# Cross-attention with a mixture of experts on one core: short clears on GpSimd behind each row transfer, and a wait ahead of every second result transfer

## The chip, the cores and the metric

The kernel runs on one core of a Trainium2 chip. Its engines work side by side and wait for each other through semaphores: TensorE (PE, with its weight loads as PEld), VectorE (DVE), ScalarE (ACT), GpSimd (POOL) and SyncE (SP). The metric is the device time of one execution in microseconds, the lower the better. A comparison is given as a ratio with an interval.

## What is computed

All numbers are float32. There are 64 sequences of 64 tokens with 256 features, so 4096 tokens. A layer norm is followed by cross-attention of each sequence over its context and itself, and by a mixture of 32 experts of which each token uses 4, beside a shared feed-forward network. Both parts are added to the residual.

```
x = x + attention(layernorm(x), keys/values = [ctx, layernorm(x)], wq, wk, wv, wo)
h = layernorm(x)
probs = softmax(h @ router.T);  topv, topi = top_k(probs, 4);  topv /= sum(topv)
out = sum over the 4 chosen experts e:  topv_e * ((silu(h @ w_gate[e]) * (h @ w_up[e])) @ w_down[e])
shared = (silu(h @ sw_gate) * (h @ sw_up)) @ sw_down
x = x + out + sigmoid(h @ sgate_w) * shared
```

An expert is 256 by 96 (gate and up) and 96 by 256 (down). The shared network is 512 wide.

## The kernel before

The tokens are cut into 16 blocks of 256 (two tiles of 128 rows) and, for the shared network, into 8 groups of 512. Each engine has its own program, written out by hand. The order on an engine is that of its code, and nothing but semaphores orders the engines among each other.

**Attention.** A loop over n runs from block to block as a pipeline: in step n, TensorE computes the projections of block n (line 806, three products for each, of a high and a low part), the attention of block n-1, the transposes and the router's logits of block n-3 (line 1012), and the places of the tokens in the experts' lists for block n-4 (lines 1021 and 1023). ScalarE copies the logits out of PSUM (line 616), and VectorE makes of them the four experts, their weights (line 1289, semaphore `weights_ready`) and the row in DRAM to which each token's copy goes (`slot_ready`). The last four steps of the loop, n = 16 to 19, carry the shared products of group 0 in place of projections. The shared products of groups 1 to 3 stand behind the loop (lines 806 and 850), and behind them the experts begin.

**The row transfers.** For each block GpSimd issues eight indirect DMAs, one for each of two tiles and four choices, which scatter 128 rows of 268 words from the buffer `rows` to `sent` in DRAM (line 481). It waits for `weights_ready`, `slot_ready` and two more of that block. `rows` is a ring of six blocks, so block b+6 is normalized into it only when the transfers of block b have landed. There are 128 such transfers. Behind some of them GpSimd runs `breathe`: it clears one of four small tiles `pause` (128 by 24, line 490), each clear waiting for the clear four before it. In the loop on GpSimd this is one clear, and only where n > 16. The transfers left behind the loop have three clears each. By the code 92 transfers have none, 24 have one and 12 have three.

**The experts.** The sorted rows make 136 tiles of 128, worked through as 68 pairs. SyncE may load from `sent` only when all row transfers have landed and the tables are made (lines 417 and 419). TensorE's loop for a pair is: transposes of pair + 2 (line 1049), transposes of the activations of pair - 1 (line 1111), gate and up products of pair + 1 (line 1100, and 1096 for pairs whose first tile mixes four experts), and the down product of pair - 3 (line 1128, and 1125 for the mixed ones), whose last matmul raises `worked_psum`. ScalarE applies silu (line 737), VectorE multiplies (line 1580), copies the transposed activations (line 1586) and scales the down product into `down_e` (line 1597, `down_ready`), a ring of four pairs that it refills once both transfers of the pair four before have landed. The call `worked(pair)` is the count at which the down product of that pair is done.

**The result transfers.** For each pair GpSimd waits for `back_ready` and `down_ready`, and then issues two indirect DMAs from `down_e` to `returned` in DRAM (line 512), one right behind the other. When all have landed, SyncE loads them back in 16 pieces, VectorE folds them into the residual (lines 1698, 1701 and 1705), and TensorE runs the shared products of groups 4 to 7 beside that (lines 806, 850 and 840).

## Time and profile before

| what | us |
|---|---|
| median of 3 runs | 516.37 (515.13 to 516.96) |
| profiled execution, its span | 667.5 |
| of that, PE busy | 574.4 |
| DVE busy | 363.5 |
| ACT busy | 288.7 |
| POOL busy | 269.4 |

The profiled execution is one execution, taken with the hardware profiler. Its span is the only time of it that is at hand, and it is 151 us longer than the median of the runs. So a time that is read in the trace can't be taken over to the runs one to one. Times in the trace count from the start of the span. "Idle before" in a row is the time that the engine waited ahead of the instruction, and the name behind the arrow is the instruction that released it. "remote" and "issue" mean that the trace shows no such instruction at that time.

### The profile page before, as it was taken

The page shows a single profiled execution, that of the slowest core. Times are in us where ns is not written, and L with a number is a line of the kernel's source. Part 1 is how long each engine was busy: PE and PEld are TensorE (multiplying, and loading weights), DVE is VectorE, ACT ScalarE, POOL GpSimd, SP SyncE. Part 2 cuts the span into 40 slices and gives each one's busy share as a digit, 9 for nine tenths or more (in the row PEclk, how much of TensorE's full clock was granted, in tenths as well). Part 3 has the DMA queues.
Part 4 walks back from the last instruction along what each step waited for, and adds up shares of the span by engine and source line. Part 5 has one row for each costly group of instructions (what it writes and reads, how often), then busy time and mean ns, then how long its engine had stood idle before and what let it go on. Part 6 is the DMA issues. An engine that isn't in the chain of part 4 may idle for free. (4 is left out here: it accounts for less than half of the span.)

```text
span 667.5 us, 13365 instructions
## 1 busy us (share of the span) xinstructions
PE 574.4 (86%) x3945; PEld 478.3 (72%) x3945; DVE 363.5 (54%) x1199; ACT 288.7 (43%) x719; POOL 269.4 (40%) x344
## 2 busy tenths in 40 slices
PE   8998787788887777899998988778877898979998
PEld 7997777677777565677886666656666676658886
DVE  5575455555555351565553635445454444536998
ACT  5775444555444440613463545444454544401111
POOL 1004444445555458380034544445454454560000
PEclk9999788987778788699997977988989978989999
DMA  5573544444433322293145444544444544228996
GB/s 160 181 227 128 170 156 129 144 134 145 138 123 113 110 76 107 70 244 98 31 130 148 131 140 124 140 136 139 130 140 140 150 131 132 87 86 330 368 340 230
DMA packets 65956, 100.77 MB, mean 151 GB/s; under 512 B 9856, under 2 KB 52864, under 8 KB 65792
## 3 DMA queue, kind: packets, MB, share of 16 engines
q1 hardware_dynamic: 48704, 60.30, 30.6%
q0 software_dynamic: 12672, 35.41, 14.7%
q10 hardware_dynamic: 4512, 4.23, 1.9%
q8 instruction: 34, 0.56, 0.4%
q14 instruction: 34, 0.28, 0.1%
HBM read 55.92 MB, written 43.97 MB: 150 GB/s over the span
## 5 line engine op out<-in xcount | busy, mean ns | idle before, releaser
L512 POOL DMA_INDIRECT returned<-arena,back x136 | 130.6, 960 | 171.7 <-DVE back L1629 81.5
L481 POOL DMA_INDIRECT sent<-rows,slot x128 | 129.9, 1015 | 159.2 <-issue 82.7
L1100 PE MATMUL bank<-w_gu,arena 128*128 x416 | 94.7, 363 | 26.6 <-issue 16.6
L1100 PEld LDWEIGHTS bank<-w_gu,arena 128*128 128x128 f32 x416 | 73.0, 205 | 32.8 <-issue 32.8
L1580 DVE TENSOR_TENSOR arena<-bank,arena 128x192 f32<-128x192 f32 x68 | 24.2, 356 | 113.5 <-ACT arena L737 94.5
L737 ACT ACTIVATE arena<-bank 128x192 f32<-128x192 f32 x68 | 22.3, 329 | 127.0 <-remote 70.5
L806 PE MATMUL bank<-w_hi_all,att_split 128*128 128x256 f32 x256 | 56.8, 314 | 18.6 <-issue 18.6
L1597 DVE TENSOR_SCALAR arena<-bank,back_to 128x256 f32<-128x256 f32 x136 | 59.0, 476 | 6.3 <-remote 5.3
L806 PE MATMUL bank<-att_split,w_hi_all 128*128 128x256 f32 x256 | 55.5, 336 | 1.4 <-issue 1.3
L710 ACT COPY hnt<-w_gu 128x384 f32 x128 | 55.7, 509 | 0.0
L806 PEld LDWEIGHTS bank<-w_hi_all,att_split 128*128 128x128 f32 x256 | 42.4, 208 | 18.2 <-issue 18.2
L806 PE MATMUL bank<-hnt_rounded,ws_hi 128*128 128x512 f32 x160 | 51.0, 412 | 2.6 <-issue 2.6
L806 PEld LDWEIGHTS bank<-att_split,w_hi_all 128*128 128x128 f32 x256 | 47.7, 248 | 4.7 <-issue 4.6
L539 ACT ACTIVATE act_t<-bank 128x512 f32<-128x512 f32 x24 | 14.2, 598 | 82.9 <-PE bank L806 66.6
L1049 PE MATMUL bank<-ident_r,loaded 128*128 128x128 f32 x272 | 46.0, 295 | 0.4 <-issue 0.4
L850 PE MATMUL bank<-ws_d,act_t 128*128 128x256 f32 x192 | 43.3, 381 | 1.0 <-DVE act_t L1241 1.0
L731 ACT COPY arena<-bank 128x512 f32<-128x512 f32 x68 | 39.5, 582 | 8.9 <-PE bank L1049 2.5
L850 PEld LDWEIGHTS bank<-ws_d,act_t 128*128 128x128 f32 x192 | 36.1, 190 | 6.4 <-DVE act_t L1241 1.4
L806 PEld LDWEIGHTS bank<-hnt_rounded,ws_hi 128*128 128x128 f32 x160 | 31.6, 197 | 10.9 <-issue 4.0
L1049 PEld LDWEIGHTS bank<-ident_r,loaded 128*128 128x128 f32 x272 | 32.6, 148 | 9.0 <-issue 2.8
L806 PE MATMUL bank<-w_lo_all,att_split 128*128 128x256 f32 x128 | 30.3, 310 | 6.8 <-issue 6.5
L1311 DVE TENSOR_REDUCE negmax<-bank 128x2 f32<-128x256 f32 x16 | 6.7, 422 | 51.8 <-remote 51.8
(216 smaller groups left out, 1128.6 us busy)
## 6 DMA issues: line engine op xcount, KB each, us to landing
arena<-returned SPq DMA_DIRECT2D x16, 1024.0 KB, 7.2
loaded<-sent SPq DMA_DIRECT2D x104, 134.0 KB
w_gu<-w_gate_up SPq DMA_DIRECT2D x32, 192.0 KB
sent<-rows SPq DMA_DIRECT2D x4, 1072.0 KB, 6.2
loaded<-sent SPq DMA_DIRECT2D x128, 33.5 KB
resid<-x SPq DMA_DIRECT2D x16, 256.0 KB, 2.9
att_plain<-ctx_t SPq DMA_DIRECT2D x16, 256.0 KB, 3.1
out<-resid ACTq DMA_DIRECT2D x7, 512.0 KB, 4.9
```

The lines of the kernel that those rows point to most:

```text
L481: pool.indirect_dma_start(out=sent, out_offset=bass.IndirectOffsetOnAxis(ap=slot[:, 2 * b + j, k:k + 1], axis=0), in_=rows[:, u, j, :], in ...
L512: pool.indirect_dma_start(out=returned, out_offset=bass.IndirectOffsetOnAxis(ap=back[:, t:t + 1], axis=0), in_=down_e[u][:, s, :], in_offs ...
L539: act.activation(act_t[:, f, :], gate_banks[f % 2][:, :], ACT.Silu) \
L710: last = act.copy(gu_copy[:, q, :, :], w_gu[:, :, bass.ds(copied_e[pair][q], 1), :] .rearrange("p c e f -> p c (e f)"))
L731: act.copy(gt[pair % 2].rearrange("p s c q -> p (s c q)"), gt_banks[pair % 2][:, :]) \
L737: act.activation(act_e[pair % 2], gu_views[pair % 2][:, :, 0:F], ACT.Silu) \
L806: last = pe.matmul(out_view, stationary(s_part, c), moving(m_part, c), start=(n == 0 and c == 0), stop=(n == 2 and c == DC - 1))
L850: last = pe.matmul(sum_banks[t // 2][:, 256 * (t % 2):256 * (t % 2) + 256], act_t[:, f, P * t:P * t + P], ws_d[:, f, :], start=(f == 0 and ...
L1049: last = pe.transpose(gt_banks[pair % 2][:, at:at + P].bitcast(F32R), loaded[:, u, s, P * c:P * c + P], ident_r[:, :])
L1100: last = pe.matmul(view[:, s, :], rows_t[:, s, c, :], w_gu[:, c, bass.ds(e[s - 2 + len(e)], 1), :] .rearrange("p e f -> p (e f)"), start=( ...
L1580: dve.tensor_tensor(act_e[pair % 2], gu_views[pair % 2][:, :, F:2 * F], act_e[pair % 2], ALU.mult).then_inc(S["act_e_ready"], 1)
L1597: last = dve.tensor_scalar(down_e[u][:, s, :], down_banks[pair % 2][:, D * s:D * s + D], back_to[:, pair // 2 % 4, 2 * (pair % 2) + s, 0:1 ...
```

## The change

On GpSimd alone, two things. In the attention loop each row transfer is followed by three clears of `pause`, in every step and not one clear in the last steps. In the experts the second result transfer of a pair waits until the down product of the next pair is done. The last pair has no such wait.

```diff
@@ -497,8 +497,7 @@
                 for turn in range(SENT_A_STEP):
                     if may_send(n - 6 if turn < 4 else n - 5):
                         send()
-                        if n > blocks:
-                            breathe(1)
+                        breathe(3)
             while sent_now[0] < len(sends):
                 send()
                 breathe(3)
@@ -509,6 +508,8 @@
                 wait(pool, "down_ready", pair + 1)
                 for s in range(2):
                     t = 2 * pair + s
+                    if s == 1 and pair + 1 < pairs:
+                        wait(pool, "worked_psum", worked(pair + 1))
                     pool.indirect_dma_start(
                         out=returned,
                         out_offset=bass.IndirectOffsetOnAxis(ap=back[:, t:t + 1], axis=0),
```

What stands on GpSimd where the row transfers begin, before (`sent` is the DRAM buffer of the rows, `slot` the places, names in brackets are the semaphores waited for):

```order
L461 IOTA lanes_after 128x1
L463 MEMSET ones_e 32x128
L481 DMA sent<-rows,slot 131200x268 [waits named_ready,weights_ready,numbered,slot_ready,no_rows,consts]
L481 DMA sent<-rows,slot 131200x268 [waits weights_ready,named_ready,slot_ready,numbered,no_rows] x7
L481 DMA sent<-rows,slot 131200x268 [waits weights_ready,slot_ready,named_ready,numbered] x85
L490 MEMSET pause 128x24
```

The same place on GpSimd after the change:

```order
L463 MEMSET ones_e 32x128
L481 DMA sent<-rows,slot 131200x268 [waits named_ready,weights_ready,numbered,slot_ready,no_rows,consts]
L490 MEMSET pause 128x24 x3
L481 DMA sent<-rows,slot 131200x268 [waits weights_ready,named_ready,slot_ready,numbered,no_rows]
L490 MEMSET pause 128x24
L490 MEMSET pause 128x24 [waits breath] x2
L481 DMA sent<-rows,slot 131200x268 [waits weights_ready,named_ready,slot_ready,numbered,no_rows]
L490 MEMSET pause 128x24 [waits breath] x3
```

Ahead of the first clear there were 93 row transfers in a row, and now there is one. No transfer has moved past another.

On GpSimd where the last row transfers end and the result transfers of the experts begin, before:

```order
L481 DMA sent<-rows,slot 131200x268 [waits weights_ready,slot_ready,named_ready,numbered]
L490 MEMSET pause 128x24 [waits breath] x3
L512 DMA returned<-arena,back 36864x256 [waits down_ready,back_ready]
L512 DMA returned<-arena,back 36864x256
L512 DMA returned<-arena,back 36864x256 [waits down_ready,back_ready]
L512 DMA returned<-arena,back 36864x256
```

The same place after the change:

```order
L481 DMA sent<-rows,slot 131200x268 [waits weights_ready,slot_ready,named_ready,numbered]
L490 MEMSET pause 128x24 [waits breath] x3
L513 DMA returned<-arena,back 36864x256 [waits down_ready,back_ready]
L513 DMA returned<-arena,back 36864x256 [waits worked_psum]
L513 DMA returned<-arena,back 36864x256 [waits down_ready,back_ready]
L513 DMA returned<-arena,back 36864x256 [waits worked_psum]
```

The order is the same, and every second transfer now has a wait of its own for a product of TensorE.

## Rows read from the trace of the kernel before

**Rows 1.** Windows: us; busy time and instructions of each engine; granted clock; DMA.
```profile
0.00:56.00 56.00, 53.15 (x453) 49.31 (x454) 34.65 (x118) 38.66 (x97) 2.89 (x20) 1.00 0.59 188
56.00:230.00 174.00, 139.05 (x1002) 123.86 (x1002) 90.86 (x368) 80.79 (x224) 89.77 (x88) 0.82 0.42 135
230.00:300.00 70.00, 58.99 (x262) 46.09 (x261) 33.98 (x127) 24.41 (x45) 46.16 (x100) 0.88 0.41 121
300.00:337.00 37.00, 35.65 (x201) 30.68 (x200) 19.20 (x51) 15.25 (x28) 0.00 (x0) 1.00 0.28 74
337.00:602.00 265.00, 224.72 (x1754) 175.55 (x1753) 128.23 (x460) 120.73 (x313) 130.59 (x136) 0.90 0.44 130
602.00:667.50 65.50, 62.83 (x282) 52.84 (x280) 56.62 (x79) 8.84 (x14) 0.00 (x0) 1.00 0.87 321
```

**Rows 2.** Timeline of PE: start us, us, what. The logits, once a block.
```profile
51.30 1.08 PE L1012 MATMUL bank<-wr,hnt 128*128 128x33 f32 x8
60.91 1.08 PE L1012 MATMUL bank<-wr,hnt 128*128 128x33 f32 x8
76.83 1.08 PE L1012 MATMUL bank<-wr,hnt 128*128 128x33 f32 x8 [0.64 <-ACT hnt L653]
92.33 1.08 PE L1012 MATMUL bank<-wr,hnt 128*128 128x33 f32 x8 [0.79 <-ACT hnt L653]
...
217.92 1.08 PE L1012 MATMUL bank<-wr,hnt 128*128 128x33 f32 x8
```

**Rows 3.** Timeline of ACT: its copy of the logits of 60.91.
```profile
68.14 0.21 ACT L616 COPY logits<-bank 128x66 f32<-128x66 f32 x1 [5.24 <-remote]
```

**Rows 4.** Timeline of POOL: row transfers without clears.
```profile
56.22 1.24 POOL L481 DMA_INDIRECT sent<-rows,slot  x1 [52.48 <-issue]
...
64.20 0.96 POOL L481 DMA_INDIRECT sent<-rows,slot  x1 [0.30 <-issue]
65.47 0.96 POOL L481 DMA_INDIRECT sent<-rows,slot  x1 [0.30 <-issue]
71.70 0.96 POOL L481 DMA_INDIRECT sent<-rows,slot  x1 [5.28 <-DVE rows L1289]
```

**Rows 5.** Timeline of POOL: with one clear, and with three.
```profile
263.58 0.97 POOL L481 DMA_INDIRECT sent<-rows,slot  x1 [0.17 <-issue]
264.54 0.14 POOL L490 MEMSET pause<- 128x24 f32 x1
264.85 0.97 POOL L481 DMA_INDIRECT sent<-rows,slot  x1 [0.17 <-issue]
...
282.83 2.19 POOL L481 DMA_INDIRECT sent<-rows,slot  x1 [0.16 <-issue]
...
288.15 0.97 POOL L481 DMA_INDIRECT sent<-rows,slot  x1 [0.16 <-issue]
289.11 0.25 POOL L490 MEMSET pause<- 128x24 f32 x3
289.52 0.97 POOL L481 DMA_INDIRECT sent<-rows,slot  x1 [0.16 <-issue]
...
297.70 0.97 POOL L481 DMA_INDIRECT sent<-rows,slot  x1 [0.16 <-issue]
```

**Rows 6.** Timeline of ACT behind the run of 16 transfers with one clear.
```profile
268.59 0.59 ACT L653 COPY hnt<-bank 128x512 f32<-128x512 f32 x1 [16.79 <-remote]
```

**Rows 7.** Timeline of PE: down products of the experts.
```profile
336.08 1.03 PE L1128 MATMUL bank<-arena 96*128 x4
338.99 1.13 PE L1128 MATMUL bank<-arena,slot_prod 96*128 x4
341.77 1.03 PE L1128 MATMUL bank<-arena,hnt 96*128 x4
...
585.78 0.70 PE L1128 MATMUL bank<-arena,hnt 96*128 x2
593.30 1.12 PE L1128 MATMUL bank<-arena,slot_prod 96*128 x4 [3.19 <-DVE arena L1597]
```

**Rows 8.** Timeline of DVE: the copy that the product of 585.78 releases.
```profile
592.28 1.66 DVE L1597 TENSOR_SCALAR arena<-bank,back_to 128x256 f32<-128x256 f32 x4 [5.33 <-remote]
```

**Rows 9.** Timeline of POOL: result transfers near the end.
```profile
588.34 0.96 POOL L512 DMA_INDIRECT returned<-arena,back  x1 [0.30 <-issue]
589.60 0.96 POOL L512 DMA_INDIRECT returned<-arena,back  x1 [0.30 <-issue]
593.92 0.95 POOL L512 DMA_INDIRECT returned<-arena,back  x1 [3.36 <-DVE arena L1597]
...
600.24 0.96 POOL L512 DMA_INDIRECT returned<-arena,back  x1 [0.30 <-issue]
```

**Rows 10.** Timelines of SP and PE: the first load, transposes and expert product.
```profile
303.79 0.38 SPq L417 DMA_DIRECT2D loaded<-sent  x1
...
324.27 0.98 PE L1049 MATMUL bank<-ident_r,loaded 128*128 128x128 f32 x8
...
326.89 1.46 PE L1100 MATMUL bank<-w_gu,arena 128*128 x8
```

**Rows 11.** Chain of work that ended last: start us, us, what.
```profile
611.13 10.90 PE bank L806 x48
```

**Rows 12.** Timeline of DVE: product among clears, first fold, last product.
```profile
295.68 0.69 DVE L1241 TENSOR_TENSOR act_t<-bank,act_t 128x512 f32<-128x512 f32 x1 [1.85 <-remote]
...
607.73 1.23 DVE L1698 TENSOR_TENSOR arena<-arena 128x1024 f32<-128x1024 f32 x1 [2.71 <-DMA arena<-returned]
...
659.43 0.68 DVE L1241 TENSOR_TENSOR act_t<-bank,act_t 128x512 f32<-128x512 f32 x1
```

## The prediction, made before the changed kernel was run

> **What bounds the kernel now.** I read the windows first, with edges where GpSimd begins and ends its transfers [rows 1]. In the three stretches without transfers (0 to 56, 300 to 337, 602 to 667.5; 158.5 us together) the granted clock is 1.00, the 2.4 GHz level, and TensorE is busy 151.6 of 158.5 us. In the three with transfers (509 us) the clock is granted at 0.82 to 0.90, so TensorE spends part of its time at the 1.2 GHz level, and it is idle 35, 11 and 40 us. So I asked the timeline what changes when transfers begin. One matmul group stands once in every block, the logits. It comes at 51.30 and 60.91, 9.6 us apart, and then at 76.83 and 92.33, 15.5 apart, up to 217.92 [rows 2]. From 60.91 to 217.92 are ten steps, 15.7 us each. The transfers began at 56.22 [rows 4].
>
> What delays the step is in the rows around it. The logits end on TensorE at 61.99 (60.91 + 1.08), but ScalarE starts to copy them at 68.14, after an idle of 5.24 us that the trace can only call remote [rows 3]. GpSimd's run of eight transfers went from 56.22 to 66.43 [rows 4]. The same at 268.59: ScalarE waited 16.79 us, and it moved 2.8 us behind the last transfer of a run of 16, which began at 264.85 [rows 5, 6]. And at the end of the experts: the down product of 585.78 is over by 586.5, yet VectorE's copy of it starts at 592.28, again released by "remote", while GpSimd issued transfers until 590.56 [rows 7 to 9]. My reading: in this trace TensorE's signals to the other engines do not arrive while GpSimd issues transfers back to back; they come 1 to 3 us after the run ends. A step of attention then is the run (8 x 1.27 = 10.1 us) plus some 5.5 us of the chain that leads to the next run.
>
> The decisive question is how much of this the timed runs have, since they take 151 us less than the span. I sum what the delays cost in the trace. Attention: 10 x (15.7 - 9.6) = 61 us. Experts: the down products run 2.9 and 2.8 us apart before the transfers hinder (336.08, 338.99, 341.77), and 257.2 us for 67 pairs, 3.84 each, over the whole stage [rows 7]: 67 x (3.84 - 2.85) = 66 us. The stretch 230 to 300: 11 us idle, and at a granted 0.88 a quarter of the 70 us at the lower level, which costs half of 17 us: 19 us together [rows 1]. The sum is 146, and 667.5 - 146 = 521.5 us, 5 us above the median of 516.4. So the timed runs behave like the trace without the delays, bound by TensorE nearly throughout. What may be left of delays in them is small: the dense stretches could be somewhat faster unprofiled (48 matmuls of 512 columns take 10.90 us, 227 ns each [rows 11], where 512 columns at 2.4 GHz are 213, so 6% of 158 us, 9 us at most). That puts the timed run without any delay between 512 and 521, and leaves 0 to about 5 us for delays.
>
> The Trainium skill, page "Runtime: NRT & Kernel Launch", section on the preamble/postamble breakdown, says that a profile's total time and the execution time differ by some 6 us whatever the kernel. This case's numbers disagree: 667.5 against 516.4. By that rule the timed run would carry all of the delays, and the change could be worth tens of us; the measurement decides against it.
>
> **The change part by part.** *The clears.* Without a clear a transfer follows the one before after 1.27 us (64.20 to 65.47) [rows 4]. With one clear it is also 1.27 (263.58 to 264.85): the clear lies in the 0.30 us gap. With three it is 1.37 (288.15 to 289.52) [rows 5]. So the 92 + 24 transfers that had none or one each cost 0.10 us more on GpSimd, 11.6 us in all, 0.8 per block. None of that is on the path by itself: VectorE needs a block's buffer only six blocks later. Per block GpSimd needs 8 x 1.37 = 11.0 us where TensorE's undelayed step takes 9.6, so GpSimd falls behind by 1.4 us per block (before: 0.5), some 14 us at the ninth block, the last for whose buffer anyone waits, against about 3 steps (29 us) of room. It is cover until the loads of the experts. There I count: first transfer at 56.2, the 128th 127 x 1.37 = 174 us later at 230, if it never waits; before, 127 x 1.27 gives 217.5. In the trace the first load stands 6.1 us behind the last transfer (297.70 to 303.79) [rows 5, 10]; some 2 us for it to land makes 238. That is an estimate. It must be there for the first transposes, which stand 2.6 us ahead of the first expert product [rows 10]. In the timed run that product comes at 516.4 - (667.5 - 326.9 - 66) = 242, so the transposes at 239. The cover holds by about a us, where it was 14. Cost taken: 0, bounds 0 and +5.
>
> A clear might also hold up VectorE beside it. Its product of 128 by 512 takes 0.69 us at 295.68, among the triple clears, and 0.68 us at 659.43, where GpSimd is idle [rows 12], so 0 for that.
>
> Whether the clears let signals through: with one clear in the gap they did not (16.79 us of waiting [rows 6]). Where three stood (282 to 299) the step shape is different and no row proves it. In the timed run I take 0, bound -2.
>
> *The wait in the experts.* It holds 67 transfers until the next pair's down product, about 2.85 us after this pair's own. GpSimd then has, per pair, the held transfer right at that signal and the first transfer of the next pair behind it: 2 x 1.27 = 2.5 us of 2.85, in step with TensorE. Queued behind the waiting transfer on GpSimd is only the next pair's first one, whose data is ready about 1 us after the same signal (VectorE's copy), so it loses at most 0.3 us. The other one who waits is VectorE's copy into the ring of four: it needs this transfer landed 4 x 2.85 = 11.4 us after this pair's copy; the transfer now starts 2 us behind that copy rather than 1.27 and lands some 2 us later. Seven us of room: cost 0. The end of the stage: the last transfers start at 593.92, six of them in a row until 600.24 [rows 9]. Now the held one of the pair before stands at their head, seven in all, but it can start at the product's signal and not at the copy's end, 0.9 us earlier. 1.27 - 0.9 = 0.4 us later at the first fold, which VectorE already waits for by 2.71 us [rows 12]. VectorE's last product comes at 659.43 behind folds, and a shift of 0.4 has about 2 us of room on TensorE. So 0, bound +0.5.
>
> What the wait can give: in the trace it stops runs longer than two transfers, so a signal is held for 2.5 + 1 us rather than up to 10. I expect the trace's pair to fall from 3.84 to about 3.4 us, 30 us of the span. In the timed run only the 0 to 5 us that are left can be won.
>
> Sum for the timed run: 0 (clears) + 0 (wait) + 0 to 0.4 (end), on 516.4: forecast 516.2, no change.
>
> **The rivals.** *A: the timed run has a rest of the delay, and the change removes it.* TensorE's signals would be late by up to one transfer (0.96 us) here and there. For it: the trace shows the effect at full size. Against: the sum above reaches the median without it. After the change a pair's two transfers lie right behind TensorE's signal and GpSimd is idle when the next one comes. Price: of the 5 us left, plus up to 5 where the dense stretches are faster than I think, most goes: 511, at best 506.
>
> *B, slower: the backlog reaches the experts.* The clears move the last row transfer from 217.5 to 230, and my cover was 1 us. If a step of attention is shorter than 9.6 us in the timed run, or the load of the 3 MB down weights holds transfers up (one took 2.19 us in the trace [rows 5]), every us beyond goes into the start of the experts one to one. It decides from a last transfer at about 232. Price: 2 to 6 us, so 520.
>
> *C, slower: the delay is there in attention's timed steps and scales with the run.* Then each run of eight is 0.8 us longer and some 11 steps are bound by it: +9 us, 525. Against it: the same sum as above.
>
> *D: the clears do not separate the transfers at all,* and the wait is always already met. This gives 516.4, the same as my forecast.
>
> **How the numbers follow.** Forecast (with D) 0.42, A 0.31, B 0.18, C 0.09. A measurement of this kernel can tell about 0.3% from no change, 1.5 us. Same is the forecast: 0.42. Faster is A: 0.31. Slower is B and C: 0.27. The range reaches to A's 508 and to B's 522; beyond it lie A's far end and C.
>
> **What would show it.** In the profile of the changed kernel: row transfers 1.37 us apart all through attention; the logits 16 us or more apart while transfers run (if the clears let signals through, 12 or less); down products about 3.4 us apart; no more than two or three result transfers in a row; ScalarE's and VectorE's remote waits in the experts shorter. A span that falls by 20 us with a median that stays is what I expect. The forecast is wrong if the median follows the span, or if the last row transfer comes too late for the first load.

## The result, and the profile after

The changed kernel took 521.91 us (519.89 to 522.69, 4 runs), the kernel before beside it 515.75 us (512.42 to 516.96, 4 runs): 1.0136 times as long, 95% interval 1.0084 to 1.0189. It is slower, by about 6 us. The ratios of this document leave out the disturbed executions of a set, and the medians are over all of them.

The page of the changed kernel. The profiled execution took 522.01 us, its span is 519.8, 2.2 us less.

```profile
span 519.8 us, 13689 instructions
PE 506.7 (97%) x3945; PEld 431.2 (83%) x3945; DVE 363.5 (70%) x1199; ACT 287.4 (55%) x719; POOL 290.3 (56%) x668
PEclk9999999999999999998999999999999999999999
```

The same windows as in [rows 1], but cut off at this span's end (us; busy time of PE, PEld, DVE, ACT, POOL; granted clock; DMA share; GB/s):

```profile
0.00:56.00 56.00, 53.42 (x452) 49.58 (x453) 34.64 (x118) 38.71 (x97) 2.89 (x20) 1.00 0.59 188
56.00:230.00 174.00, 173.62 (x1336) 154.73 (x1335) 134.93 (x521) 109.99 (x278) 153.94 (x503) 1.00 0.59 183
230.00:300.00 70.00, 67.31 (x554) 55.42 (x553) 40.00 (x136) 39.66 (x97) 31.26 (x41) 0.98 0.54 153
300.00:337.00 37.00, 36.16 (x335) 28.76 (x333) 23.26 (x85) 24.07 (x64) 24.17 (x27) 1.00 0.62 181
337.00:519.00 182.00, 176.16 (x1276) 142.72 (x1274) 130.71 (x342) 74.97 (x186) 78.06 (x81) 1.00 0.67 225
```

Where [rows 1] has 139 busy us of 174 at a clock of 0.82, this has 173.6 at 1.00, while GpSimd is busy for 154 of the 174. The logits, to be laid beside [rows 2], come every 9.6 us (timeline of PE):

```profile
60.98 1.08 PE L1013 MATMUL bank<-wr,hnt 128*128 128x33 f32 x8
70.59 1.08 PE L1013 MATMUL bank<-wr,hnt 128*128 128x33 f32 x8
80.20 1.08 PE L1013 MATMUL bank<-wr,hnt 128*128 128x33 f32 x8
```

ScalarE copies them 0.2 us after they end, not 6 as in [rows 3], with no wait put down to "remote" (timeline of ACT):

```profile
62.21 0.22 ACT L617 COPY logits<-bank 128x66 f32<-128x66 f32 x1 [0.56 <-PE bank L1024]
```

So nothing is left of the 146 us of held signals in this trace. It looks as if the change had removed them. It had not: a profile of the unchanged kernel, taken later (before_b, below), has none either. TensorE is now 97% busy. Of the 13.1 us that it is idle, 2.6 lie in the first 56 us, and nearly all of the rest at the start of the experts and behind it. The last row transfers (timeline of POOL), the first load (SP), and TensorE beside them (PE):

```profile
230.31 0.97 POOL L481 DMA_INDIRECT sent<-rows,slot  x1 [0.16 <-issue]
231.27 0.24 POOL L490 MEMSET pause<- 128x24 f32 x3
231.68 0.97 POOL L481 DMA_INDIRECT sent<-rows,slot  x1 [0.16 <-issue]
```

```profile
235.24 0.38 SPq L417 DMA_DIRECT2D loaded<-sent  x1
```

```profile
238.18 0.50 PE L1050 MATMUL bank<-ident_r,loaded 128*128 128x128 f32 x4 [1.06 <-DMA loaded<-sent]
239.56 0.53 PE L1050 MATMUL bank<-ident_r,loaded 128*128 128x128 f32 x4 [0.88 <-DMA loaded<-sent]
239.93 3.65 PE L851 MATMUL bank<-ws_d,act_t 128*128 128x256 f32 x8
243.38 1.50 PE L1101 MATMUL bank<-w_gu,arena 128*128 x8
```

TensorE waits twice for the loads, 1.94 us. Behind that the clock falls to its 1.2 GHz level for 3.4 us (a window of the same trace, the clock is the 0.50), so the L851 group takes 3.65 us where it takes 1.96 elsewhere:

```profile
240.00:243.40 3.40, 3.40 (x11) 2.65 (x10) 0.00 (x0) 0.59 (x1) 0.00 (x0) 0.50 0.31 78
```

### The profile page after: what moved, and what is told of

Same layout as the page of the kernel before. It is cut to its first block and busy times, and to the rows that moved or that the text cites. A ratio compares the mean times of both kernels' runs of the same rounds, so it can differ in the third digit from the quotient of the medians.

```text
span 519.8 us, 13689 instructions
## 1 busy us (share of the span) xinstructions
PE 506.7 (97%) x3945; PEld 431.2 (83%) x3945; DVE 363.5 (70%) x1199; ACT 287.4 (55%) x719; POOL 290.3 (56%) x668
## 5 line engine op out<-in xcount | busy, mean ns | idle before, releaser
L481 POOL DMA_INDIRECT sent<-rows,slot x128 | 125.8, 983 | 72.6 <-issue 70.1
L1101 PE MATMUL bank<-w_gu,arena 128*128 x416 | 83.6, 338 | 0.8 <-ACT arena L732 0.4
L1101 PEld LDWEIGHTS bank<-w_gu,arena 128*128 128x128 f32 x416 | 66.0, 190 | 1.5 <-issue 1.3
L807 PE MATMUL bank<-w_hi_all,att_split 128*128 128x256 f32 x256 | 48.6, 292 | 0.0
L1050 PE MATMUL bank<-ident_r,loaded 128*128 128x128 f32 x272 | 41.7, 276 | 5.2 <-DMA loaded<-sent 5.2
L851 PE MATMUL bank<-ws_d,act_t 128*128 128x256 f32 x192 | 44.7, 391 | 0.0
L807 PE MATMUL bank<-att_split,w_hi_all 128*128 128x256 f32 x256 | 44.4, 286 | 0.0
L732 ACT COPY arena<-bank 128x512 f32<-128x512 f32 x68 | 39.6, 582 | 5.9 <-PE bank L1050 4.6
L851 PEld LDWEIGHTS bank<-ws_d,act_t 128*128 128x128 f32 x192 | 37.2, 195 | 5.4
L807 PEld LDWEIGHTS bank<-w_hi_all,att_split 128*128 128x128 f32 x256 | 37.1, 191 | 0.9 <-issue 0.9
L807 PEld LDWEIGHTS bank<-att_split,w_hi_all 128*128 128x128 f32 x256 | 37.0, 194 | 0.2
L490 POOL MEMSET pause<- 128x24 f32 x384 | 31.2, 142 | 0.0
L1097 PE MATMUL bank<-hnt,arena 128*32 128x192 f32 x512 | 27.4, 332 | 0.0
```

Of the source, the lines that this page charges most:

```text
L481: pool.indirect_dma_start(out=sent, out_offset=bass.IndirectOffsetOnAxis(ap=slot[:, 2 * b + j, k:k + 1], axis=0), in_=rows[:, u, j, :], in ...
L490: pool.memset(pause[breaths[0] % len(pause)][:, :], 0.0).then_inc(S["breath"], 1)
L732: act.copy(gt[pair % 2].rearrange("p s c q -> p (s c q)"), gt_banks[pair % 2][:, :]) \
L807: last = pe.matmul(out_view, stationary(s_part, c), moving(m_part, c), start=(n == 0 and c == 0), stop=(n == 2 and c == DC - 1))
L851: last = pe.matmul(sum_banks[t // 2][:, 256 * (t % 2):256 * (t % 2) + 256], act_t[:, f, P * t:P * t + P], ws_d[:, f, :], start=(f == 0 and ...
L1050: last = pe.transpose(gt_banks[pair % 2][:, at:at + P].bitcast(F32R), loaded[:, u, s, P * c:P * c + P], ident_r[:, :])
```

## The experiments

**Two conditions of the chip.** The kernels ran in five sets, those of a set on one chip beside the kernel before. The kernel before had a median of 515.23 us in the second set and 516.86 in the fourth, but of 653.38, 669.88 and 660.44 in the first, third and fifth. In the three long sets the traces show the held signals of [rows 3, 6]; in the two short ones there are none. I call these sets held and free. The set of the first result, above, was free too. The third (held) and the fourth (free) ran under the same chip number, eight minutes apart. Held times scatter by up to 4%, so a held ratio says less than a free one, and its median stands beside it.

**First set (held): the parts, one by one.** The clears alone:

```
-                        if n > blocks:
-                            breathe(1)
+                        breathe(3)
```

> The clears of the change alone, without the wait in the experts. Theory B (the clears push the last row transfer so far back that the experts' first loads come late): last row transfer near 231.7 us as in the profile after, TensorE waits about 1.9 us for the first loaded tiles near 237 us and then works 3 to 4 us at the lower clock, ratio to before 1.007 to 1.014. Theory W (the wait in the experts costs the time): ratio within 0.3% of 1. If the clears are what freed the signals, the logits stand under 10 us apart in its profile, and the experts, which have no clears, stay at about 3.8 us per pair.

Measured: 653.70 us (6 runs: four near 654, one at 638.6, one at 632.8) against 653.38; ratio 0.9742 (0.9665 to 0.9818), which rests on the two short ones alone. I take it as not settled.

The wait alone:

```
+                    if s == 1 and pair + 1 < pairs:
+                        wait(pool, "worked_psum", worked(pair + 1))
```

> The wait of the change alone, row transfers as before. Theory B: ratio within 0.3% of 1, last row transfer about 10 us earlier than after the change, no wait of TensorE for the first loads. Theory W: ratio 1.007 to 1.014. If the wait is what freed the signals in the experts, its profile shows attention's logits 15.5 us apart and the down products 2.8 us apart.

Measured: 630.46 us against 653.38; 0.9519 (0.9455 to 0.9583). Faster. The wait with one clear behind each row transfer:

```
-                        if n > blocks:
-                            breathe(1)
+                        breathe(1)
```

> As the change, but one clear behind each row transfer in the loop and not three; a transfer with one clear follows the one before after 1.27 us, as without any. Theory B: the backlog is gone, so ratio within 0.3% of before. Theory W: as slow as the change, 1.007 to 1.014. A third reading, that the clears themselves disturb VectorE through the memory they share: a third of the cost of the clears.

Measured: 634.16 us; 0.9626 (0.9538 to 0.9715). And the kernel before once more:

> The kernel before, unchanged, profiled a second time. If the long span of its first profile (667.5 us against 516 timed) belongs to the program as it runs under the profiler, the span is again over 600 us, with signals of TensorE held up while GpSimd issues transfers. If it was a chance of that one execution, the span is about 514 us and shows directly what the timed runs do.

Measured: 659.92 us; 1.0066 (1.0007 to 1.0125), which shows how far such a set is to be trusted: the same kernel differs from itself by 1%. Its total for ScalarE's copy of the logits (groups by line: busy, mean ns, idle before), with 61.9 us of "remote", and under it the changed kernel's in the free condition:

```profile
L616 ACT COPY logits<-bank 128x66 f32<-128x66 f32 x16 | 3.4, 215 | 63.0 <-remote 61.9 <-PE bank L1023 0.6 <-PE bank L1012 0.5
```

```profile
L617 ACT COPY logits<-bank 128x66 f32<-128x66 f32 x16 | 3.5, 216 | 5.1 <-PE bank L1024 4.4 <-PE bank L1013 0.5
```

So timed runs of 650 us have the held signals of [rows 1 to 9] in full: they belong to the execution and not to the profiler. The result transfers of the experts, in before_again and then in wait_only (timeline of POOL):

```profile
499.64 0.96 POOL L512 DMA_INDIRECT returned<-arena,back  x1 [0.30 <-issue]
500.90 0.96 POOL L512 DMA_INDIRECT returned<-arena,back  x1 [0.30 <-issue]
502.17 0.96 POOL L512 DMA_INDIRECT returned<-arena,back  x1 [0.30 <-issue]
505.07 0.96 POOL L512 DMA_INDIRECT returned<-arena,back  x1 [1.94 <-DVE back L1629]
```

```profile
503.70 0.96 POOL L514 DMA_INDIRECT returned<-arena,back  x1 [0.31 <-issue]
505.80 0.96 POOL L514 DMA_INDIRECT returned<-arena,back  x1 [1.13 <-remote]
507.88 0.96 POOL L514 DMA_INDIRECT returned<-arena,back  x1 [1.12 <-DVE arena L1599]
509.14 0.97 POOL L514 DMA_INDIRECT returned<-arena,back  x1 [0.30 <-issue]
```

From the first result transfer to the last are 246.9 us in before_again (341.1 to 588.0) and 224.6 in wait_only (341.6 to 566.1). Attention is nearly the same in both: last row transfer at 291.0 and 291.7. The 22 us lie in the experts.

**Second set (free): the same parts.** The kernel before:

> The kernel before once more, to see which of two kinds of execution this chip gives. Theory: whether TensorE's signals are held while GpSimd issues transfers belongs to the chip or its condition, not to the program. Where before is timed near 516 us, its profile has a span near 514 us, logits 9.6 us apart throughout attention and no signal held; where it is timed near 655 us, the span is near 653 us and the logits stand 15 us apart. The rival, that the profiler makes the difference, expects a span over 640 us beside a time of 516.

Measured: 515.38 us (510.32 to 519.51, 10 runs); 0.9989 (0.9942 to 1.0036). The clears alone:

> The clears alone. On a chip where before takes near 516 us: theory B (the clears push the last row transfer back until the first loads come late) expects a ratio of 1.007 to 1.014 and TensorE waiting about 1.9 us for the first loaded tiles; theory W (the wait in the experts costs the time) expects 1.000. On a chip where before takes near 655 us: 0.97 again.

Measured: 520.85 us (519.88 to 523.02, 6 runs) against 515.23; 1.0118 (1.0060 to 1.0175). The wait alone:

> The wait alone. On a chip where before takes near 516 us: theory B expects a ratio within 0.3% of 1, last row transfer near 220 us, TensorE not waiting for the first loads; theory W expects 1.007 to 1.014. On a chip where before takes near 655 us: 0.95 again.

Measured: 515.03 us; 1.0006 (0.9965 to 1.0047). In the free condition the clears carry the cost and the wait costs nothing. TensorE at the start of the experts, in before_b and then in clears_b (timeline of PE):

```profile
235.01 0.98 PE L1049 MATMUL bank<-ident_r,loaded 128*128 128x128 f32 x8
235.84 1.96 PE L850 MATMUL bank<-ws_d,act_t 128*128 128x256 f32 x8
237.63 1.46 PE L1100 MATMUL bank<-w_gu,arena 128*128 x8
```

```profile
236.65 0.51 PE L1048 MATMUL bank<-ident_r,loaded 128*128 128x128 f32 x4 [0.90 <-DMA loaded<-sent]
238.21 0.53 PE L1048 MATMUL bank<-ident_r,loaded 128*128 128x128 f32 x4 [1.05 <-DMA loaded<-sent]
238.57 1.96 PE L849 MATMUL bank<-ws_d,act_t 128*128 128x256 f32 x8
240.37 0.81 PE L1099 MATMUL bank<-w_gu,arena 128*128 x4
```

**Third set (held), meant to tell lateness from clears.** With four clears on the 24 transfers that the kernel before gives one, and none added elsewhere:

```
                         if n > blocks:
-                            breathe(1)
+                            breathe(4)
```

> The kernel before, with no clear behind the first 92 row transfers (as before) and four clears instead of one behind the next 24, those that GpSimd issues while attention's last blocks end; no wait in the experts. Three clears make 1.37 us between transfers (0.96 of issue, 0.41 of clears), so four make 1.51 against 1.27 with one: 24 x 0.24 = 5.8 us later for the last row transfer, the same delay as in clears_b (230.3 against 224.2), though attention itself has not one clear more than before. If the clears cost because the last row transfer is late (my theory): ratio 1.012, 521 us on a chip where the kernel before takes 515, experts' first product at 240. If they cost inside attention (a lengthened step, a port that VectorE shares with GpSimd during attention): 1.002 or less. On a chip where TensorE's signals are held, about 1.00.

Measured: 663.81 us against 669.88; 1.0008 (0.9946 to 1.0070). One more register load for each pair on SyncE:

```
+                nc.values_load_multi_w_load_instructions(
+                    tile_row[0:1, first:first + 1], ...
                 wait(sp, "turned_psum", pair - RING + 1)
```

> The kernel before, with one more register load of one value on SyncE for each pair of the experts (its value is not used). In the traces of before_b, wait_b and clears_b SyncE never waits from its first load of a tile to its last: 185.6, 195.2 and 193.4 us of issuing, with 68 register loads of 0.5 us (two values) or 1.1 (five), so 0.2 a value and 0.1 for the instruction. The addition is then 68 x 0.3 = 20 us of SyncE. If SyncE's issuing paces the experts (my theory for the waits for loads in the middle of the experts): loads lead their use by 5 to 6.5 us at the start, of which 3 to 4 can be used up before TensorE waits, so +16 to +20 us, ratio 1.035, many waits of TensorE for loads. If SyncE has room and the waits come from the transfers themselves (bandwidth shared with the result transfers): under 1.005.

Measured: 671.91 us; no ratio. This kernel turned out to be the kernel before: the register was not used, and the added load does not stand in the trace, which has 68 of them as before. One and two clears (`breathe(1)` and `breathe(2)` behind every transfer in that loop), with the wait:

> One clear behind each row transfer of attention in place of none or one (the last twelve keep three), and the wait in the experts. One clear lies in the gap of 0.30 us between two transfers, so the last row transfer stands where it stood before (224 to 225). If the cost of the change is the late last transfer: 1.000 (0.997 to 1.003) where the kernel before takes 515; on a chip where it takes 653 about 0.962, as measured once. If any clear costs something in attention: 1.003 to 1.006.

> As one_clear_wait_b, with two clears. Two clears are 2 x 0.137 = 0.27 us, still within the gap of 0.30 us: the last row transfer at 224 to 226 and a ratio of 1.000 (0.997 to 1.004). If the cost grows with the number of clears from the first one on (a third of 1.2% for each): 1.008.

Measured: 644.05 us, 0.9705 (0.9603 to 0.9806), and 643.08 us, 0.9644 (0.9510 to 0.9779). The gain of the wait came again. What I wanted to tell apart is hidden in this condition.

**Fourth set (free): the same again, and the changed kernel.**

> Four clears instead of one behind the 24 row transfers after attention's blocks, none added before; no wait. The last row transfer is then 24 x 0.24 = 5.8 us later than in before_b, at 230. If the lateness is the cause: 1.012 where the kernel before takes 515 (521 us). If clears cost inside attention: under 1.003. On a chip where the kernel before takes over 640: 1.000, as in late_clears (1.0008).

Measured: 518.75 us (12 runs) against 516.86; 1.0029 (1.0003 to 1.0054). This missed what was expected of lateness, 1.012 with the last row transfer at 230. The transfer came at 226.9: the space between two transfers (median, in the traces) is 0.305 us with no clear or one, 0.345 with two, 0.40 with three and 0.45 with four, so four clears cost 0.15 us and not 0.24. So the last transfer stood 1.3 us later than in slow_sp_c and 2.7 later than in before_b (table below), not 5.8, and the small cost of this run can't by itself tell lateness from clears.

> One more register load of one value on SyncE for each pair of the experts, some 0.3 us each, 20 us of SyncE in all. If SyncE's issuing paces the experts: +16 to +20 us (1.035) where the kernel before takes 515, with waits of TensorE for loads all along. If the transfers' bandwidth does: under 1.005. Where the kernel before takes over 640 TensorE is slower than SyncE (pairs of 3.6 us and more) and the addition is hidden: 1.00, and the trace must show SyncE waiting there.

Measured: 516.80 us; 0.9982 (0.9950 to 1.0013): the kernel before against itself, no test of SyncE.

> Two clears behind each row transfer and the wait in the experts. 0.27 us of clears in a gap of 0.30 us: last row transfer at 224 to 226, ratio 1.000 (0.997 to 1.004) where the kernel before takes 515. If each clear costs a third of the 1.2%: 1.008. Where the kernel before takes over 640: 0.964, as in two_clears_wait.

Measured: 517.73 us; 1.0025 (0.9994 to 1.0057). The last row transfer came at 226.9 and not at 224 to 226, since two clears do not fit into the 0.305 us.

> The changed kernel. Where the kernel before takes 515: 1.013, as in its first measurement. Where it takes over 640: the wait gives 4.8% and the clears 2.6% alone, and both shorten the same held signals, so less than their sum: 0.94 to 0.955.

Measured: 522.55 us (8 runs); 1.0089 (1.0049 to 1.0130). With the first measurement, 0.9 to 1.4% slower.

The eight profiles of the free condition, one to a row. The first four columns are us after TensorE's last logits product, since one trace may begin 2 us earlier than another; the fifth is the stretch from SyncE's first load of a tile to its last; the sixth is the sum of what these 232 issues took beyond 0.35 us each; the seventh is TensorE's idle time ahead of the transposes of loaded tiles, over all pairs. The last two are the time of the profiled execution, and the kernel's median less that of the kernel before beside it.

| kernel | last row transfer | first load | first expert product | last transposes | SyncE's loads | long issues | TensorE waits | its time | median difference |
|---|---|---|---|---|---|---|---|---|---|
| before_b | 38.2 | 41.9 | 51.6 | 236.3 | 185.6 | 4.9 | 0.0 | 510.3 | +0.2 |
| slow_sp_c (= before) | 39.6 | 43.2 | 51.6 | 240.0 | 191.2 | 11.9 | 2.1 | 513.7 | -0.1 |
| wait_b | 39.6 | 43.1 | 51.6 | 243.4 | 195.2 | 14.1 | 4.6 | 517.2 | -0.2 |
| two_clears_wait_c | 41.0 | 44.5 | 51.6 | 244.4 | 194.9 | 14.5 | 4.5 | 518.2 | +0.9 |
| late_clears_c | 40.9 | 44.5 | 51.6 | 245.0 | 195.7 | 15.3 | 4.6 | 518.9 | +1.9 |
| clears_b | 43.9 | 47.5 | 54.0 | 246.5 | 193.3 | 14.9 | 7.3 | 521.8 | +5.6 |
| after_c | 44.0 | 47.6 | 54.0 | 247.9 | 192.9 | 13.3 | 8.8 | 523.0 | +5.7 |
| changed, first profile | 43.9 | 47.5 | 55.6 | 246.3 | 193.8 | 13.8 | 5.2 | 522.0 | +6.2 |

The last column rises with the first. late_clears_c and two_clears_wait_c have the same lateness, one from 3 more clears on 24 transfers and the other from up to two more on 116, and cost the same within their intervals, though costs as small as these tell little. At 1.4 us of lateness (against wait_b) the cost is 1 to 2 us, at 4.3 us 5.6 to 6.2 us.

That the clears do not cost inside attention is shown by the traces more sharply: from the first row transfer to the start of TensorE's last logits matmul are 131.5 us in each of the eight, with no clear, with two and with three (in the changed kernel 56.27 to 187.76). So up to there the clears lengthen nothing. The first difference stands behind it, where the loads are late.

So the loss has these parts. The one that is shown is the start: the first expert product comes 2.4 us later in clears_b and after_c, and 4.0 in the first profile, where the clock fell there. A second is the granted clock: a mean of 0.997 or less, which one fall of 3.4 us gives, stands in 12 of the 18 runs of the changed kernel and of clears_b, and in 11 of the 76 free runs of the kernel before that list it. With two falls in three of the 18 and 1.7 us for each fall, this is an estimated 1.2 us of the mean difference, part of it at the start. Some 2 us are left for the experts. TensorE's waits ahead of transposes, less the 1.9 us at the start, are 3.3 to 6.9 us in clears_b, after_c and the first profile, and 0 to 4.6 us in before_b, slow_sp_c and wait_b. These ranges overlap, so one profile of each kernel does not settle this part. The rows of it in wait_b and then in clears_b (groups by line: busy, mean ns, idle before):

```profile
L1051 PE MATMUL bank<-ident_r,loaded 128*128 128x128 f32 x272 | 41.7, 277 | 4.6 <-DMA loaded<-sent 4.5
```

```profile
L1048 PE MATMUL bank<-ident_r,loaded 128*128 128x128 f32 x272 | 41.6, 276 | 7.3 <-DMA loaded<-sent 7.2
```

One line's instructions in the changed kernel and then in before_b: the second load of each pair, from the first to the last, and who waited.

```profile
L419 SPq DMA_DIRECT2D loaded<-sent x68: 332/348/1732, 235.8 to 429.0; - x68
its engine sat idle before it (us, times) until:
who waited for it (us, times):
  PEld bank L1050: 9.1, 14
  PE bank L1050: 5.2, 8
```

```profile
L419 SPq DMA_DIRECT2D loaded<-sent x68: 332/351/1637, 228.5 to 413.5; - x68
```

SyncE waits for nothing from its first load of a tile to its last, in any of the eight (0.3 us once in before_b): it loads registers, issues, and goes on. In before_b the last load of a pair is issued 4.5 to 8.4 us ahead of TensorE's transposes of it; in the changed kernel 2.2 to 4.5 us for most pairs, and TensorE stops where the lead is 2.2 to 2.5 or an issue is long. But this is not the change's doing alone: the lead is as short, 2.5 to 4.5 us for most pairs, in slow_sp_c and wait_b, whose first load is on time, and before_b is the exception. A load issue takes 0.33 us, but one in some 16 takes up to 2.1; as that adds up to 5 us or to 12 to 15, SyncE is just quick enough for TensorE, or is not. The long ones are not strewn by chance: outside before_b they come mostly every 11 to 16 issues, and some places are the same in all seven traces (the 64th or 65th issue, the 135th or 136th). Whether they are SyncE's own or the transfers behind it hold them up, no run tells. A queue that never waits has no time to catch up in, so a late first load stays late. That is how I read it; it is argued and not shown, and a run that changes only SyncE's time was still wanted. The Trainium skill, page "DMA: Bandwidth & Descriptors", section "Rules for kernel authors", says that spreading DMAs over several issuing engines brings no bandwidth and saves only the sequencer's issue time. No run here tried that. By this reading it is the issue time that is short.

**Fifth set (held), the last.** Five clears on the 24 transfers; an extra register load whose value addresses each pair's second load; and no clear at all (both `breathe` calls behind transfers taken out), with the wait.

```
                         if n > blocks:
-                            breathe(1)
+                            breathe(5)
```

> Five clears instead of one behind the 24 row transfers that follow attention's blocks, none added before them, no wait. Four made these 24 take 34.0 us in late_clears_c (31.3 in before_b); one more clear each is 24 x 0.14 = 3.3 us: the last row transfer at about 230, as in clears_b and after_c (230.3, 229.9). If its lateness is the whole cause: 1.010 to 1.012 where the kernel before takes 515. If clears in attention are part of it: 1.003 to 1.006.

```
+                _, again = nc.values_load_multi_w_load_instructions(
+                    tile_row[0:1, first + P // size:first + P // size + 1], ...
-                sp.dma_start(loaded[:, u, 1, :].bitcast(F32), sent[bass.ds(at[P // size], P), :])
+                sp.dma_start(loaded[:, u, 1, :].bitcast(F32), sent[bass.ds(again[0], P), :])
```

> The kernel before; SyncE reads the row number of each pair's second tile once more, in a register load of its own, and addresses the second load by it: 68 more register loads of at least 0.3 us, 20 us or more of SyncE's time in the experts. If SyncE's issuing paces the experts (it never waits there, and loads lead their use by 3 to 7 us): 3 to 5 us are taken by the lead and the rest comes through, +15 to +25 us, ratio 1.03 to 1.05, with waits of TensorE for loads in nearly every pair. If SyncE's time has room: under 1.005.

> No clear at all behind row transfers of attention (the last twelve had three, 24 before them one), and the wait in the experts. The last twelve come 0.10 us closer each: last row transfer 1.2 us earlier than in wait_b and slow_sp_c (225.3), at 224. If the time follows the last row transfer below that point too: 0.997 to 0.999 where the kernel before takes 515. If there is a threshold that 225 does not pass: 1.000 to 1.001.

Measured, against 660.44: late_five 637.66, 0.9708 (0.9633 to 0.9782); slow_sp2 658.85, 1.0048 (0.9952 to 1.0144); no_clears_wait 632.24, 0.9621 (0.9556 to 0.9685). The set was held, so the first two answer nothing about the free condition. slow_sp2 has its 68 added register loads:

```profile
L419 SPq TENSOR_LOAD <-arena x68: 3/274/706, 293.1 to 539.1; - x68
```

Some 20 us of SyncE, and no cost seen, because here SyncE has time: from 340 us on it waits 28.8 us for VectorE in before_again and 6.4 in slow_sp2. no_clears_wait repeats the gain of the wait. That late_five gained 3% where late_clears gained nothing is a result that I can't explain: the two differ by one clear on 24 transfers, and ran in different sets.

## Why the prediction was wrong

**The step that failed** is the cost of the clears: "The cover holds by about a us, where it was 14. Cost taken: 0, bounds 0 and +5." Three of its terms can be set against rows.

- *The last row transfer.* Forecast 230, measured 231.68, or 229.9 and 230.3 in the two other profiles. Right. Before I had it at 217.5 and it is at 224.2 to 225.3, for without clears the issues themselves are sometimes longer, 1.14 and 1.37 us (before_b, timeline of POOL):

```profile
121.47 1.14 POOL L481 DMA_INDIRECT sent<-rows,slot  x1 [0.30 <-issue]
122.91 1.14 POOL L481 DMA_INDIRECT sent<-rows,slot  x1 [0.30 <-issue]
124.35 1.37 POOL L481 DMA_INDIRECT sent<-rows,slot  x1 [0.30 <-issue]
```

All 128 of them in before_b and then in the changed kernel (busy, mean ns):

```profile
L481 POOL DMA_INDIRECT sent<-rows,slot x128 | 130.9, 1023 | 84.7 <-issue 83.2 <-ACT rows L589 0.8 <-DVE rows L1289 0.8
```

```profile
L481 POOL DMA_INDIRECT sent<-rows,slot x128 | 125.8, 983 | 72.6 <-issue 70.1 <-ACT rows L590 1.5 <-DVE rows L1290 0.2
```

  The issues give back 5.1 us of the 11.6 that I summed for the clears, so the last transfer moved by about 5 us (4.3 to 5.8 in the table) and not by the 12.5 between my two figures. Only the 230 was right.
- *When the load is needed.* I worked out 239 from a sum of held delays; TensorE's transposes stand ready at 235.0 (before_b). This is the mis-sized term: 4 us. Some 2.2 us of it are that I put the median of 516.4, a device time, where a span was needed, which is 2.2 us shorter. The first load follows the last transfer by 3.6 us and not by 6.1, which took over half of the error back. The cover was not +1 but about -1.5 us: TensorE begins the transposes at 236.5 (after_c) in place of 235.0.
- *What a late start costs.* I let it cost itself at most, in rival B "one to one". At the start it did less than that, 2.4 us of 4.3, or 4.0 with the drop of the clock, for which I had no term. The whole cost, 5.6 to 6.2, is more than one to one. The rest came behind the start, in part by falls of the clock; that SyncE's queue has no slack there is my reading of it.

**Rival B** was right in kind and nearly in place: "the backlog reaches the experts' first loads", price 2 to 6 us, 520. But neither of the two conditions that I gave for it held: the step is 9.6 us, and no load of weights held the transfers up past 230. The loads were needed sooner than I thought. It decides not from a last transfer at 232 but below 230, and perhaps before 227, where late_clears_c loses 2 us and two_clears_wait_c 1 (the latter could be nothing, by its interval). I gave it 0.18.

**The timed run and the trace.** "What the delays cost" came to 146 us, and 667.5 - 146 = 521.5 was near the median. The kind of it was right: the free profile of before has a span of 508.0, logits 9.6 us apart and the clock at 1.00. The size was some 7 us short, since a run of 516.4 has a span of 514.2, and 667.5 is 153 above that. The reason was wrong. I took the held signals for something that only the profiled execution had. They are a condition in which every run of a set is long, and the profile of before, by its rows, was taken in this one and the times beside it in the other. In one execution the time is the span and 2.2 us more (522.01 and 519.8; 510.32 and 508.0). So I was right to set aside the gap of some 6 us (the Trainium skill, page "Runtime: NRT & Kernel Launch", section "The ~15µs preamble/postamble breakdown") as a way from 667.5 to 516.4, but the two numbers were never one execution's, and no rule for a gap could be judged by them. One execution's numbers differ from that page too: 2.2 us and not some 6, with the span as the shorter one, though the page's total may take in more than the span. Taking the held signals for the profiler's own left me the "rest of the delay" that rival A, 0.31, lived on: the free traces have none to win.

**Rival C** needed delays in attention's timed steps. None in the free condition. **D** is out by clears_b and the three clears in the rows.

**The wait.** Cost 0, bound +0.5: right, 1.0006 (0.9965 to 1.0047). Two steps of that working hold in rows of the changed kernel. The last transfers lie 1.27 us apart up to the last at 453.16, and the first fold waits 4.07 us for data, on VectorE, of which TensorE feels 0.17 (timelines of POOL, DVE, PE):

```profile
451.89 0.96 POOL L513 DMA_INDIRECT returned<-arena,back  x1 [0.30 <-issue]
453.16 0.96 POOL L513 DMA_INDIRECT returned<-arena,back  x1 [0.30 <-issue]
```

```profile
460.71 1.23 DVE L1699 TENSOR_TENSOR arena<-arena 128x1024 f32<-128x1024 f32 x1 [4.07 <-DMA arena<-returned]
```

```profile
472.64 0.73 PE L807 MATMUL bank<-hn_hi,ws_hi 128*128 128x512 f32 x2 [0.17 <-DVE act_t L1242]
```

"I expect the trace's pair to fall from 3.84 to about 3.4 us": in the held sets the 67 pairs take 224.6 to 227.4 us with the wait (wait_only, one_clear_wait, one_clear_wait_b, two_clears_wait, no_clears_wait), 3.35 to 3.39 each, and 246.2 to 256.2 without it (before_again, clears_only, late_clears, slow_sp, late_five, slow_sp2). The size was right, and in such a set it is real time, 3 to 5%. That runs of transfers keep TensorE's signals back, and that breaking the runs lets them through, agrees with this for the experts. In attention three short clears did not let them through: the logits are 15.5 us apart on average in clears_only as in before_again, and ScalarE's copy of them still waits 48.1 us for "remote", against 61.9. The last row transfer comes at 289.5 with three clears beside 291.0 without (first set), and at 299.3 with two beside 296.3 without (third set, slow_sp).

**Expected of the changed profile** were row transfers 1.37 us apart (they are), logits 16 us apart or 12 (9.6), pairs of 3.4 (about 2.9) and a span 20 us shorter with an unchanged median (148 us shorter than that of [rows 1], with a median 6 us up). All but the first describe the other condition.

**Left open:** how much of the loss behind the start is SyncE's issue time, since its test was never run in the free condition; what makes an issue long; what makes a chip hold the signals; why late_five gained there; and how the changed kernel itself does there. It was not measured in a held set. From its parts it would be faster, and that is an inference.

## What to carry to other kernels

A trace whose span is not the time of the runs beside it may be of another condition, not of another instrument: compare each execution's time with its own span before anything is subtracted, and profile the kernel before again beside the changed one. Where a queue's last item releases the next stage, work added to every item of the queue arrives there as a sum, and "hidden beside other work" has to be shown at that last item, to the us. Then look whether the stage behind it has slack anywhere: a late start can cost more than the lateness, as here 5.6 to 6.2 us for 4.3, and I take a queue that never waits for the sign of it. The wait alone, without the clears, was as fast as the kernel before where that takes 515 us and 3 to 5% faster where it takes 650.

## What the runs showed of the hardware

- TensorE's signals were held back while GpSimd issued indirect transfers in three sets of five, 650 to 670 us, and not at all in the two others and in that of the first result, 515 to 517 us, with the same kernel; one chip number had both. In the free traces the issues are as dense, 8 in 9.9 to 11.2 us, and all 128 stand one behind the other without the pause of some 5 us that follows most runs of eight in the held ones.
- An indirect transfer's issue (0.96 us) with nothing behind it but the next one is sometimes 1.14 or 1.37 us and up to 1.9 (26 of 128 over 1.05 us in before_b, mean 1023 ns); with three clears behind each 5 of 128, mean 983. One clear (0.14 us) lies in the 0.305 us between two transfers; two made it 0.345, three 0.40 and four 0.45.
- SyncE's issue of a tile's load takes 0.33 us, and about one in 16 up to 2.1, mostly every 11 to 16 issues. The sum of the excess differs between executions of the same kernel, 4.9 and 11.9 us, and their times by 3.4 us (before_b and slow_sp_c). I take the spread of the kernel before, 510 to 519 us, to be mostly this.
- In the first profile of the changed kernel the granted clock was 0.50 for 3.4 us after waits of 1.06 and 0.88 us; in clears_b waits of 0.90 and 1.05 us at the same place, and in after_c of 1.20 and 0.72, had no fall behind them. In clears_b, after_c, two_clears_wait_c and late_clears_c it also fell once for 3.4 us, at another place in each, 0.1 to 1.1 us behind the end of a single wait of 1.3 to 1.5 us; in before_b, slow_sp_c and wait_b waits of 1.3 us stood without a fall behind them. So the length of a wait does not tell whether a fall follows. One fall costs 1.7 us.
